# Delta-net stage of a two-layer perceiver: outputs scaled tile by tile on ScalarE, decays scaled by a reciprocal, decay sums in quarters

## The reference, cut to what matters

```python
q = _l2norm(q) * DK ** (-0.5)
k = _l2norm(k)
g = -jnp.exp(A_log) * jax.nn.softplus(a + dt_bias)
beta = jax.nn.sigmoid(b)
...
def step(state, inp):
    qt, kt, vt, gt, bt = inp
    state = state * jnp.exp(gt)[..., None, None]
    kv = jnp.einsum('bhk,bhkv->bhv', kt, state)
    delta = (vt - kv) * bt[..., None]
    state = state + jnp.einsum('bhk,bhv->bhkv', kt, delta)
    out = jnp.einsum('bhk,bhkv->bhv', qt, state)
    return (state, out)
...
var = jnp.mean(jnp.square(o), axis=-1, keepdims=True)
o = o * jax.lax.rsqrt(var + EPS) * norm_w
o = o * jax.nn.silu(z.reshape(Bn, Sn, HV, DV))
return o.reshape(Bn, Sn, VAL_DIM) @ W_out.T
```

## Time and profile before

| what | value |
|---|---|
| time, median of 3 runs | 1522.33 us (1520.09 to 1527.14) |
| profiled execution, own time | 1516.5 us |
| its span, first to last instruction | 1514.5 us |
| mean granted TensorE clock | 0.976 of full |
| busy in the span: PE, DVE, ACT, POOL | 1406.5, 1097.7, 602.0, 612.8 us |
| delta net loop, 616 to 1156 us, 540 us: PE, DVE, ACT, POOL busy | 527.6, 489.2, 278.5, 358.1 us |

### The profile page before, as it was taken

The page is one execution under the profiler, slowest core; times in us unless marked ns, Lnnn a source line. Parts: engine busy times, 40 slices in busy tenths (PEclk is TensorE's granted clock), DMA queues, the critical chain, the costliest instruction groups (busy, mean ns, idle before and its releaser), DMA issues. The chain is left out here.

```text
span 1514.5 us, 32607 instructions
## 1 busy us (share of the span) xinstructions
PE 1406.5 (93%) x13504; PEld 971.8 (64%) x13504; DVE 1097.7 (72%) x1710; ACT 602.0 (40%) x1012; POOL 612.8 (40%) x935
## 2 busy tenths in 40 slices
PE   6999499999997878999999999999999888999999
PEld 3444278877885446667676667777666664655556
DVE  3898576687557778988999999888998645433443
ACT  2444253355324434455545455544555321111110
POOL 1021143244214646666766656766666610000000
PEclk9999799999998999999999999999999999999999
DMA  8443300110000132122122112122212105000000
GB/s 247 157 132 91 70 1 2 29 29 2 1 1 1 32 80 50 46 44 59 44 56 52 44 43 60 43 56 53 46 41 52 38 15 223 1 1 0 14 1 14
DMA packets 125955, 74.63 MB, mean 49 GB/s; under 512 B 95536, under 2 KB 107056, under 8 KB 124016
## 3 DMA queue, kind: packets, MB, share of 16 engines
q1 hardware_dynamic: 125808, 72.55, 18.3%
HBM read 54.68 MB, written 17.83 MB: 48 GB/s over the span
## 5 line engine op out<-in xcount | busy, mean ns | idle before, releaser
L1888 DVE SCALAR_TENSOR_TENSOR W<-PS,wc,W 128x504 f32<-128x504 f32 x375 | 271.1, 732 | 36.4 <-ACT W L1581 27.3
L2218 PE MATMUL PS<-HT,wgu 128*128 128x512 f32 x320 | 143.5, 592 | 0.0
L1581 ACT ACTIVATE W<-PS,wc 128x512 f32<-128x512 f32 x125 | 85.9, 688 | 136.0 <-PE PS L1282 83.8
L1282 PE MATMUL PS<-HT,wv 128*128 128x512 f32 x252 | 120.0, 607 | 8.8 <-DVE W L1888 8.8
L2352 DVE SCALAR_TENSOR_TENSOR act<-th,PS 128x512 f32<-128x512 f32 x48 | 33.0, 686 | 128.3 <-ACT th L2278 128.3
L1469 PE MATMUL PS<-wo,ogT 128*128 128x256 f32 x512 | 117.0, 387 | 7.3 <-DVE dl L1959 5.1
L1305 PE MATMUL PS<-wz,HT 128*128 128x256 f32 x512 | 121.1, 389 | 0.0
L1282 PE MATMUL PS<-HT,wkq 128*128 128x512 f32 x248 | 118.2, 620 | 2.9 <-DVE W L1888 2.9
L1469 PEld LDWEIGHTS PS<-wo,ogT 128*128 128x128 f32 x512 | 99.1, 194 | 21.8 <-DVE dl L1959 5.3
L2278 ACT ACTIVATE th<-PS 128x512 f32<-128x512 f32 x48 | 28.7, 597 | 206.6 <-PE PS L2218 206.6
L1305 PEld LDWEIGHTS PS<-wz,HT 128*128 128x128 f32 x512 | 95.3, 192 | 17.6 <-issue 4.0
(11 more groups left out here) (277 smaller groups left out, 2950.9 us busy)
## 6 DMA issues: line engine op xcount, KB each, us to landing
a_rows<-AT SPq DMA_DIRECT2D x16, 512.0 KB, 3.0
wk<-in_l0x_k SPq DMA_DIRECT2D x16, 384.0 KB, 5.7
wgu<-in_moe_gu SPq DMA_DIRECT2D x5, 1024.0 KB, 16.3
queries_scratch<-tts SPq DMA_DIRECT2D x32, 128.0 KB, 2.5
wkq<-in_gdn_w SPq DMA_DIRECT2D x16, 256.0 KB, 3.3
wv<-in_gdn_w SPq DMA_DIRECT2D x16, 256.0 KB, 2.9
wz<-in_gdn_w SPq DMA_DIRECT2D x16, 256.0 KB, 2.7
wo<-in_gdn_w SPq DMA_DIRECT2D x16, 256.0 KB, 3.1
```

Of the source, the lines that this page charges most:

```text
L1282: mm = pe.matmul(PS[:, qbank(h, q), :], w[:, o:o + DK], HT[:, k, f * 512:(f + 1) * 512], start=(k == 0), stop=(k == DC - 1))
L1581: a.activation(acc[:, flows(h, q), :], PS[:, qbank(h, q), :], ACT.Copy, scale=wc[:, h % 2, 4 * c + 3:4 * c + 4]).then_inc(s["tap"], 1)
L1888: v.scalar_tensor_tensor(a0, p0, wc[:, h % 2, 4 * c + 2 - k:4 * c + 3 - k], a0, ALU.mult, ALU.add).then_inc(s["conv"], 1)
L2218: mm = pe.matmul(PS[:, 2 * (i % 2) + w, :], pack[:, k, w, :], HT[:, k, f * N:(f + 1) * N], start=(k == 0), stop=(k == DC - 1))
```

## The change

Five edits in `phase3`.

1. `scale_out` is new on ACT: 8 activations of 128x128, each with a per-partition scale `ms[:, hv, n]`, scale `dl` in place. In `step(j)` it stands for value head 0 between `decays(h)` and `tap(h, 2)`, for value head 1 between `tap(h, 2)` and `tap(h, 3)`. In `last()` both stand ahead of `keep_out(g, 0)`. At the end value head 0 stands between `scale_wo(LAST)` and `keep_out(LAST, 0)`. The two multiplies of `dl` on POOL go.
2. `factors` loses its power and square for k: DVE takes `rk = 1 / nm` after `norms`. The norm of k, `sk`, is one power with exponent 0.5 after `Et`. The power and square for q go.
3. The norm of q is no longer multiplied in: `eq = 1e-6 * nm` of q is made on DVE, and `level` is one instruction instead of two. `gates` on POOL keeps only the power.
4. `decay_sums(h)` for h > 0 is 16 matmuls of 64x64 by 128, one for each quarter of the columns, each half of the partitions and each value head, instead of 2 of 128x128 by 512. Value head 1 uses the other partition half as source, so its log decays are swapped once at the start, by two activations into `gs` on ACT.
5. `pick` on POOL takes three small copies instead of two.

```diff
@@ decay_sums, TensorE
-                        pe.matmul(PS[:, 6 + hv, :], C("after"), flat(gm[:, hv, :, :]), start=True, stop=True).then_inc(s["dps"], 1)
+                        if h == 0:
+                            pe.matmul(PS[:, 6 + hv, :], C("after"), flat(gm[:, hv, :, :]), start=True, stop=True).then_inc(s["dps"], 1)
+                    if h > 0:
+                        for c in range(4):
+                            for b in range(2):
+                                for hv in range(2):
+                                    r, w = slice(64 * b, 64 * b + S), slice(place(hv, b), place(hv, b) + S)
+                                    mm = pe.matmul(PS[r, 6 + hv, c * P:(c + 1) * P], C("after")[w, w], flat(gm[w, hv, :, :])[:, c * P:(c + 1) * P],
+                                                   start=True, stop=True)
+                        mm.then_inc(s["dps"], 2)
@@ ScalarE
+                def scale_out(g, hv):
+                    a.wait_ge(s["fz"], g + 1)
+                    a.wait_ge(s["gz"], g * 2 + 2 - hv)
+                    for n in range(TILES):
+                        x = a.activation(dl[:, hv, n, :], dl[:, hv, n, :], ACT.Copy, scale=ms[:, hv, n:n + 1])
+                    x.then_inc(s[f"og{hv}"], 1)
@@ step(j), ScalarE
                     decays(h)
+                    scale_out(g, 0)
                     tap(h, 2)
+                    scale_out(g, 1)
                     tap(h, 3)
                     keep_out(g, 0)
@@ after last(), ScalarE
                 scale_wo(LAST)
+                scale_out(LAST, 0)
                 keep_out(LAST, 0)
@@ factors(h), GpSimd
-                    g.wait_ge(s["nm"], h + 1)
-                    kh, qh = slice(0, TILES), slice(TILES, 2 * TILES)
-                    g.tensor_tensor(rr[:, par, kh], nm[:, kh], C("mhalf")[:, kh], ALU.pow).then_inc(s["rr"], 1)
-                    g.wait_ge(s["rr"], h * 7 + 1)
-                    g.tensor_tensor(r2[:, par, kh], rr[:, par, kh], rr[:, par, kh], ALU.mult).then_inc(s["rr"], 1)
-                    g.wait_ge(s["rr"], h * 7 + 2)
+                    g.wait_ge(s["rk"], h * 2 + 1)
                     for hv in range(2):
-                        g.tensor_tensor(dd[:, hv, :], gj[:, par, :, 2 + hv], r2[:, par, 0:TILES], ALU.mult).then_inc(s["rr"], 1)
+                        g.tensor_tensor(dd[:, hv, :], gj[:, par, :, 2 + hv], rk[:, par, :], ALU.mult).then_inc(s["rr"], 1)
...
-                    g.tensor_tensor(rr[:, par, qh], nm[:, qh], C("mhalf")[:, qh], ALU.pow).then_inc(s["rr"], 1)
-                    g.wait_ge(s["rr"], h * 7 + 6)
-                    g.tensor_tensor(r2[:, par, qh], rr[:, par, qh], rr[:, par, qh], ALU.mult).then_inc(s["rr"], 1)
+                    g.tensor_tensor(sk[:, par, :], nm[:, 0:TILES], C("phalf"), ALU.pow).then_inc(s["rr"], 1)
@@ gates(j), GpSimd
-                    g.wait_ge(s["fz"], j * 2 + 1)
-                    g.tensor_tensor(ms[:, :, :], ms[:, :, :], over(rr[:, j % 2, TILES:2 * TILES], 2), ALU.mult).then_inc(s["fz"], 1)
-                    g.wait_ge(s["fz"], j * 2 + 2)
-                    for hv in range(2 if j < LAST else 1):
-                        g.wait_ge(s["gz"], j * 2 + 2 - hv)
-                        g.tensor_tensor(dl[:, hv, :, :], dl[:, hv, :, :], each(ms[:, hv, :], DK), ALU.mult).then_inc(s[f"og{hv}"], 1)
@@ norms(h) and level(j), VectorE
+                    v.wait_ge(s["nm"], h + 1)
+                    v.reciprocal(rk[:, h % 2, :], nm[:, 0:TILES]).then_inc(s["rk"], 1)
+                    v.tensor_scalar(eq[:, h % 2, :], nm[:, TILES:2 * TILES], 1e-6, None, ALU.mult).then_inc(s["rk"], 1)
...
-                    v.tensor_tensor(ms[:, :, :], ms[:, :, :], over(r2[:, j % 2, TILES:2 * TILES], 2), ALU.mult).then_inc(s["ms"], 1)
-                    v.wait_ge(s["ms"], j * 4 + 3)
-                    v.tensor_scalar(ms[:, :, :], ms[:, :, :], 1.0 / (4 * DK * DK), 1e-6, ALU.mult, ALU.add).then_inc(s["ms"], 1)
+                    v.scalar_tensor_tensor(ms[:, :, :], ms[:, :, :], 1.0 / (4 * DK * DK), over(eq[:, j % 2, :], 2), ALU.mult, ALU.add).then_inc(s["ms"], 1)
```

More of the change, by code:

```diff
@@ L61, in shape_constants @@
     put("mhalf", np.full((P, 32), -0.5))
+    put("phalf", np.full((P, 8), 0.5))
     put("ones", np.ones((P, 1)))
@@ L1075, in phase3 @@
         gm = sb(ctx, "gm", [P, 2, TILES, S])
+        gs = sb(ctx, "gs", [P, TILES, HK])
         E = sb(ctx, "E", [P, 2, TILES, S])
@@ L1085, in phase3 @@
         nm = sb(ctx, "nm", [P, 2 * TILES])
-        rr = sb(ctx, "rr", [P, 2, 2 * TILES])
-        r2 = sb(ctx, "r2", [P, 2, 2 * TILES])
+        rk = sb(ctx, "rk", [P, 2, TILES])
+        eq = sb(ctx, "eq", [P, 2, TILES])
         sk = sb(ctx, "sk", [P, 2, TILES])
@@ L1103, in phase3 @@
         ms = sb(ctx, "ms", [P, 2, TILES])
-        s = semaphores(ctx, "ab_mm ab_v ab_a ab_p ab_b ab_g ab_r win vin zin cin oin nin nws pj tap conv th y zz zt z2 u16 qq kk dg nr nm rr gj gm dps e ed et av pd "
-                            "d1 sin sub d3 t16 x xs yy tu mt zs ct mss o us ms gz fz og0 og1 ogt ogs wo xa todd wof vt vc zero sx gin nst nrt nap", "p3_")
+        s = semaphores(ctx, "ab_mm ab_v ab_a ab_p ab_b ab_g ab_r win vin zin cin oin nin nws pj tap conv th y zz zt z2 u16 qq kk dg nr nm rr rk gj gm dps e ed et av pd "
+                            "d1 sin sub d3 t16 x xs yy tu mt zs ct mss o us ms gz fz og0 og1 ogt ogs wo xa todd gsw wof vt vc zero sx gin nst nrt nap", "p3_")
         NQ = 8
@@ L1307, in project_z, with place @@
                     mm.then_inc(s["zz"], 1)
+                def place(hv, b):
+                    return 64 * b if hv == 0 else 64 * (1 - b)
                 def decay_sums(h):
@@ L1356, in turn_v @@
                     mm.then_inc(s["vt"], 1)
-                def place(hv, b):
-                    return 64 * b if hv == 0 else 64 * (1 - b)
                 def cross(j):
@@ L1618, in square_o @@
                     if j > 0:
-                        a.wait_ge(s["ms"], j * 4 - 3 + hv)
+                        a.wait_ge(s["ms"], j * 3 - 2 + hv)
                     a.activation(so[:, hv, :], wide(obank(hv)), ACT.Square).then_inc(s["us"], 1)
@@ L1632, in swap_scale @@
                 def swap_scale(h):
-                    a.wait_ge(s["rr"], h * 7 + 5)
+                    a.wait_ge(s["rr"], h * 3 + 3)
                     if h > 1:
@@ L1704, in _ @@
                 tanh(0, 6)
+                other = ga[:, :, 0:HV].rearrange("p n (k two) -> p n k two", two=2)[:, :, :, 1]
+                a.wait_ge(s["ab_g"], 1)
+                a.activation(gs[64:P, :, :], other[0:64], ACT.Copy)
+                a.activation(gs[0:64, :, :], other[64:P], ACT.Copy).then_inc(s["gsw"], 1)
                 tanh_z(0, 0)
@@ L1769, in pick @@
                 def pick(h):
-                    g.tensor_copy(gj[:, h % 2, :, 0:2], ga[:, :, 2 * h:2 * h + 2]).then_inc(s["gj"], 1)
+                    g.tensor_copy(gj[:, h % 2, :, 0:1], ga[:, :, 2 * h:2 * h + 1])
+                    g.tensor_copy(gj[:, h % 2, :, 1:2], gs[:, :, h:h + 1]).then_inc(s["gj"], 1)
                     g.tensor_copy(gj[:, h % 2, :, 2:4], ga[:, :, HV + 2 * h:HV + 2 * h + 2]).then_inc(s["gj"], 1)
@@ L1854, in _ @@
                 factors(0)
+                g.wait_ge(s["gsw"], 1)
                 pick(1)
@@ L1914, in norms @@
                     if h > 0:
-                        v.wait_ge(s["rr"], h * 7)
+                        v.wait_ge(s["rr"], h * 3)
                     v.wait_ge(s["dg"], h * 2 + 2)
@@ L1951, in sum_o @@
                     if hv == 0 and j > 0:
-                        v.wait_ge(s["fz"], j * 2)
+                        v.wait_ge(s["fz"], j)
                         v.wait_ge(s["og1"], j)
@@ L1962, in level @@
                 def level(j):
-                    v.wait_ge(s["ms"], j * 4 + 2)
-                    v.tensor_tensor(ms[:, :, :], ms[:, :, :], over(r2[:, j % 2, TILES:2 * TILES], 2), ALU.mult).then_inc(s["ms"], 1)
-                    v.wait_ge(s["ms"], j * 4 + 3)
-                    v.tensor_scalar(ms[:, :, :], ms[:, :, :], 1.0 / (4 * DK * DK), 1e-6, ALU.mult, ALU.add).then_inc(s["ms"], 1)
+                    v.wait_ge(s["ms"], j * 3 + 2)
+                    v.wait_ge(s["rk"], j * 2 + 2)
+                    v.scalar_tensor_tensor(ms[:, :, :], ms[:, :, :], 1.0 / (4 * DK * DK), over(eq[:, j % 2, :], 2), ALU.mult, ALU.add).then_inc(s["ms"], 1)
                 def step(j):
@@ L2078, in last @@
                     gate(j, 0)
-                    v.wait_ge(s["fz"], j * 2 + 2)
+                    v.wait_ge(s["fz"], j + 1)
                     v.wait_ge(s["gz"], j * 2 + 2)
```

5 lines of the change are left out of this document (2 added, 3 removed).

## The result

| | time, us | runs |
|---|---|---|
| before | 1521.19 median (1515.41 to 1527.14) | 6 |
| changed | 1559.65 median (1557.58 to 1562.37) | 6 |
| changed / before | 1.0251, 95% interval 1.0222 to 1.0281 | |

The change costs 38.5 us. The forecast was 1552, within 1534 to 1572. The profiled execution of the changed kernel has a span of 1555.8 us, 41.3 more than the one of before.

What follows compares the result with a forecast made beforehand. ACT's queue was taken to set the stretch from decay sums to `scores`: 24 + 4.5 + 1 (clock) + 1 - 1 + 0.5 = +30 us, predicting 1552 on the median's footing of 1522.33, range 1534 to 1572.

Steps and rivals of the forecast that it cites:

- What bounds the step: Delta net loop: ACT's queue delays the taps and so `scores`, 1.7 us a step, +24 us; chance 0.64.
- the front: Stretch of a loop step from decay sums to `scores`: mean 12.31 us before, forecast 14.0 in every step.
- S: Time of eight scaling activations on ACT for one value head: 2.25 us, bounds 2.1 and 3.2.
- The collision: In the loop, GpSimd's scaling of `dl` slows a DVE `silu` to 2.19 us; without it 0.69.
- The clock: Lower TensorE clock behind the longer wait at the end: +1 us; none counted in the loop.
- rival B: Clock also falls in the loop behind the new wait ahead of `turn_out`: 1577, or 1565 if half the steps; chance 0.15.
- The back: Stretch of a loop step from `scores` to the next decay sums: held fixed at 32.74 us, no new wait.
- Decay sums in quarters: Decay sums on PE: 0.99 us instead of 1.72, the saving turning into waiting, worth 0.
- Decays by reciprocal, level, pick, head 0: Small edits on POOL and DVE: +1 us in the loop, -1 for head 0, `pick` 0, 0.5 in `last()`.
- The end: Last head's scaling on ACT stands behind `scale_wo(LAST)`, which waits for a DMA: `project_out` later, +4.5 us.
- Step 1: First loop step, taken as the others: 1.7 us lost.

Runs made afterwards that it cites:

- e5: Changed kernel with each scaling as one 128x1024 activation using the first tile's scale, so seven tiles of eight lack the right scale: 1519.7 us.
- e2: Changed kernel with both scalings moved behind `tap(h, 3)` in ACT's queue in `step(j)`: 1578.0 us.
- e3: Changed kernel with the multiplies of `dl` back in `gates` on GpSimd and `scale_out` called nowhere, other edits kept: 1517.9 us.
- e4: Changed kernel with the decay sums again as two full 128x128 by 512 matmuls and `pick` as before: 1564.6 us.
- e8: e6 with the decay sums as two full matmuls instead of quarters: 1523.2 us.
- e1b: Changed kernel with the last `scale_out` ahead of `scale_wo(LAST)` instead of behind it, a repeat for a profile: 1553.7 us.
- e6: Changed kernel with value head 0 scaled on VectorE, head 1 on ScalarE behind `tap(h, 3)`, last scaling ahead of the output weights' scaling: 1509.5 us.
- e7: e6 with two of the eight tiles of value head 1 also scaled on VectorE: 1508.9 us.
- e9: e4 with the decay sums made twice over in every step but the first, filling TensorE's wait: 1557.0 us.
- e10: Changed kernel with `cross(j)` ahead of `turn_out(g, 0)` instead of behind it, meant to cut TensorE's wait in two: 1559.6 us.

## Why the prediction was right, and where it was off

- *What bounds the step.* Right. The stretch that matters is the front, and ACT's queue sets it: `tap(h, 2)` starts at +6.74 (6.75 forecast) and, in the undisturbed steps, `scores` at +14.08 (14.0), DVE last to release it. "In every step alike" was wrong: the fallen clock makes the fronts 14.07 to 16.24 and the period 47.89 instead of 46.7. e5, which changes nothing but the activations' time, takes the loss away; e2 shows that it isn't the order alone.
- *S, the time of a scaling.* Forecast 2.25, measured 2.34 from start to start. The activations start 0.293 apart, and the surcharge that I took for SBUF as source was too small. The estimate from the figures of the Trainium skill ("ScalarE: Activation LUTs", "What ACT_TABLE_LOAD costs") was 2.34, and this trace agrees. It made no difference to `tap(h, 2)`, by luck: the exponentials, which end at +4.61 before, end at +4.52 now, because the decay sums, the zero of this count, start 0.1 us later against everything else.
- *The collision.* Right: silus at about 0.69 in every step of the loop; e3 brings the 2.38 back. The Trainium skill ("SBUF — State Buffer", "Who interferes with whom") has a VectorE instruction with two SBUF inputs contend with a GpSimd instruction that reads SBUF. Both traces agree: 2.38 us beside GpSimd's multiply, 0.69 without it.
- *The clock: the term that was mis-sized.* The sum had 1 us for it, at the end alone, and made falls in the loop rival B (0.15). Measured: 10 us in steps 2 to 13, 2 in step 14, and some 2 at the end, 14 in all. These 13 us over the term are more than the whole 8.5 by which the rise exceeds the forecast. The step that failed is "Against it: step 6 already has a wait there and granted clock 1.00". It also misreads the rows: in step 6 of the kernel before, `turn_out` has no wait. The wait stands behind both of them, ahead of `project(h, 4)`, and is 1.35 us long, against the new one of 2.11. Rival B's mechanism came true on top of A, in 8 of the 13 steps 2 to 14: in six at 1.9 to 2.2 us, near the 1.8 a step that B had, in two at 0.26. TensorE, step 6 before:

```profile
803.63 1.95 PE L1282 MATMUL PS<-HT,wv 128*128 128x512 f32 x4 [1.35 <-DVE W L1888]
```

- *The back.* Taken as fixed at 32.74, it came out at 33.08 behind undisturbed fronts. It comes with the other edits and not with the scaling on ACT: e3, which scales on GpSimd, has 33.04. About 0.1 us is the step into the 64x64 matmuls of the decay sums (`turn_v` to decay sums 0.53 instead of 0.44 us), the rest short waits of `project_z` (L1307) for DVE of 0.2 us. Forecast +1 in all, measured +2.6.
- *Decay sums in quarters.* 1.03 us forecast as 0.99, worth nothing behind ACT's wait: right by e4 (front 14.16 against 14.08). e8 shows what they are worth once that cover is gone: 0.3 us a step in the period, not the 0.73 that the PE work would give.
- *Decays by reciprocal, level, pick, head 0.* The start of the delta net is 1.1 us shorter (1 forecast), and e3's time shows no cost. Its back, 0.3 us a step longer, does, and a front 0.2 shorter pays for most of it; which of the edits brings which wasn't tested one by one.
- *The end.* The place behind the DMA: 4.5 forecast, 4.8 by e1b. Right. The clock behind it, 1 forecast, cost about 1.9.
- *Step 1.* Counted as +1.7, measured +0.6. There `turn_out` is late in both kernels, at +12.79 before and at +11.72 now.
- *Sum.* Forecast +30, measured +38.5 on the medians and +41.3 in the profiled execution. In the profiled execution the undisturbed fronts and step 1 make 23.9 (24 forecast), the back 2.6 (1), the end without its clock 4.9 (4.5 and 0.5), the start -1.1 (-1), the clock 14 (1). The stages ahead, -3.3, are in no term of the sum, so 3 us of the nearness to the forecast are luck.

What stays open: the exact condition under which the clock falls. In this study it fell behind waits of 2.11 us in some steps and not in others with the same rows. It did not fall behind e3's longest wait in steps 2 to 14, 1.73 us ahead of `project(h, 4)`, nor behind the 0.54 and 0.56 of e6; in e4 it fell behind 1.67 ahead of `turn_out`, and in e7 once behind 0.54 and then 1.44. In e4 every third step falls, and in e2 every third is spared, with the same wait to within 0.2 us. So the length of one wait doesn't decide it, and that e9's matmuls keep the clock up is shown by one profiled execution.

## What to carry to other kernels

An engine that is 52% busy can still have no room: what counts is the stretch of its queue between the result it waits for and the one that others wait for. Put work of no urgency behind the instructions that feed another engine, and ahead of an instruction that waits for a DMA, and split it over the engines that stand idle in that stretch. Moving it alone only exchanged who waits (e2); splitting it paid (e6). When a change makes TensorE wait longer, count the slower matmuls behind the wait too.

## What the runs showed of the hardware that I had not expected

- With the full decay sums, waits of 1.67 us ahead of the transposes and up to 0.76 behind `cross` let the clock fall in 4 of 13 steps; with 2.11 it fell in 8 (twice for 0.26 us only), with 3.25 in 9, with two waits of about 0.5 in none, and with 0.77 and 0.40 (e9) in none. Where it counts, a fall costs about 1.9 to 2.3 us in the changed kernel and e4, up to 3.0 in e2 and e7, and mostly about 1 in e10. Redundant matmuls in the wait (e9) removed the falls, and the front rose by 0.15 us over e4's undisturbed one.
- The decay sums in quarters: 32 records of 64x64 by 128 pass in 1.03 us against 1.72 for the 4 records of the full sums. They start 0.03 us apart, where the transposes' records, also of 128 columns but 128x128, start 0.12 apart, so the four quarters ran side by side, as forecast. Ahead of the first stand 0.1 us.
- The power on GpSimd takes 2.9 us for 16 columns, 1.6 to 2.0 for 8, 1.0 for 4. Dropping a power of 8 columns, the small multiplies behind the powers and both multiplies of `dl` freed 79 us of GpSimd in the loop, and the loop was not shorter for it.
